# VectorE's attention loop written out, with the normalised row moved between the limit and the factors

## The reference

```
xm = exp(layer_norm(log(x)) * (1 + scale) + shift)
q, k, v = to_heads(exp(log(xm) @ w + b))          # 16 heads of 16, norms per head
out = exp(softmax(log(q) log(k)^T / 4) @ log(v))  # 64 x 64 scores per sequence and head
z = exp(log(from_heads(out)) @ w_o + b_o)
x1 = mobius_add(x, exp(gate * log(z)))
the same frame again around w_f1 and w_f2 (an MLP without an activation), then x + result
```

## Time and profile before

| what | us |
|---|---|
| time, median of three runs | 818.61 (817.21 to 820.23) |
| time of the profiled execution | 816.74 |
| its span, first to last instruction | 815.0 |
| DVE busy in the span | 671.9 (82%) |
| PE busy | 655.6 (80%) |
| ACT busy | 531.5 (65%) |
| POOL busy | 337.5 (41%) |
| mean granted clock of TensorE, share of full | 0.940 |

### The profile page before, as it was taken

The page is one execution under the profiler, slowest core; times in us unless marked ns, Lnnn a source line. Parts: engine busy times, 40 slices in busy tenths (PEclk is TensorE's granted clock), DMA queues, the critical chain, the costliest instruction groups (busy, mean ns, idle before and its releaser), DMA issues.

```text
span 815.0 us, 27718 instructions
## 1 busy us (share of the span) xinstructions
PE 655.6 (80%) x8355; PEld 468.1 (57%) x8369; DVE 671.9 (82%) x2230; ACT 531.5 (65%) x1563; POOL 337.5 (41%) x682
## 2 busy tenths in 40 slices
PE   5966988888888888888888887714669889989996
PEld 2655766666666666666666665502326556556654
DVE  2868898888889888888888898486997888888885
ACT  1125666667766666776666776334777888878884
POOL 1004555555555555555555555211233233134231
PEclk9979999999999999999999999555999999999999
DMA  9933755565555555565555654322443455445533
GB/s 322 357 98 89 137 130 119 131 134 124 134 129 129 123 129 134 123 133 118 129 128 125 133 132 98 76 65 65 117 117 102 125 150 155 131 130 155 152 96 104
DMA packets 184931, 107.53 MB, mean 132 GB/s; under 512 B 140202, under 2 KB 167730, under 8 KB 184883
## 3 DMA queue, kind: packets, MB, share of 16 engines
q1 hardware_dynamic: 183090, 104.11, 51.7%
q10 hardware_dynamic: 1792, 2.89, 1.0%
HBM read 64.24 MB, written 9.18 MB: 90 GB/s over the span
## 4 chain that ended last, share of the span: by engine, by line
DVE 34%; issue 29%; PE 15%; DMA 8%; DVEq 5%; ACT 4%; SPq 3%; POOL 2%; POOLq 0%; ACTq 0%
DVE hs L1151 7%; DVE lnx L1078 4%; PE p_s L948 3%; DVE g_all L1180 3%; DVEq L50 3%; SPq L365 3%; DMA mod_b<-mod_rows 2%; DMA qkT<-mod_b 2%; PE p_oz L859 2%; DMA x_all<-in_x 2%; PE p_qkv L948 2%; DVE fac L1200 2%; PE p_qkv L886 2%; DVE junk L1187 1%; PE p_t L934 1%
## 5 line engine op out<-in xcount | busy, mean ns | idle before, releaser
L886 PE MATMUL p_qkv<-wqkv,tT 128*128 128x256 f32 x768 | 197.2, 395 | 5.6 <-DVE u L1145 5.6
L886 PEld LDWEIGHTS p_qkv<-wqkv,tT 128*128 128x128 f32 x768 | 139.6, 195 | 22.8 <-issue 6.5
L859 PE MATMUL p_oz<-wo,oT 128*128 128x256 f32 x256 | 79.9, 439 | 6.0 <-ACT oT L624 0.5
L900 PEld LDWEIGHTS p_o<-v,pT 64*64 64x64 f32 x4096 | 67.9, 139 | 22.6 <-issue 22.6
L853 PE MATMUL p_oz<-ident,o 128*128 128x128 f32 x128 | 27.7, 300 | 63.4 <-DVE o L1165 55.1
L900 PE MATMUL p_o<-v,pT 64*64 64x17 f32 x4096 | 74.2, 211 | 0.0
L624 ACT ACTIVATE oT<-p_oz 128x256 f32<-128x256 f32 x64 | 24.6, 384 | 70.9 <-PE p_oz L853 70.9
L666 ACT ACTIVATE pT<-p_s 128x1024 f32<-128x1024 f32 x64 | 65.5, 1024 | 2.4 <-PE p_s L876 1.4
L1145 DVE SCALAR_TENSOR_TENSOR u<-p_qkv,ct,bqkv 128x768 f32<-128x768 f32 x64 | 64.4, 1006 | 3.2 <-PE p_qkv L886 3.2
L511 POOL TENSOR_TENSOR rt<-ss,c_mhalf 128x2 f32<-128x2 f32 x32 | 24.3, 760 | 101.7 <-ACT wqkv L714 99.0
L853 PEld LDWEIGHTS p_oz<-ident,o 128*128 128x128 f32 x128 | 13.3, 145 | 85.9 <-issue 80.7
(11 more groups left out here) (268 smaller groups left out, 1674.8 us busy)
## 6 DMA issues: line engine op xcount, KB each, us to landing
mod<-mod_rows SPq DMA_DIRECT2D x128, 128.0 KB, 2.8
x_all<-in_x SPq DMA_DIRECT2D x8, 1024.0 KB, 13.9
gate<-mod_rows SPq DMA_DIRECT2D x128, 64.0 KB, 2.8
mod<-mod_rows SPq DMA_DIRECT2D x32, 256.0 KB, 3.9
mod_b<-mod_rows SPq DMA_DIRECT2D x32, 256.0 KB, 4.0
out<-x_all SPq DMA_DIRECT2D x32, 256.0 KB, 2.2
gate<-gate_rows SPq DMA_DIRECT2D x32, 128.0 KB, 3.3
bqkv<-gate_rows SPq DMA_DIRECT2D x32, 128.0 KB, 3.8
```

The source lines that it names most:

```text
L859: mm = pe.matmul(p_oz[:, 0:D], oT[:, c, :, :].rearrange("p b s -> p (b s)"), wo[:, c, :], start=c == 0, stop=c == C - 1)
L886: mm = pe.matmul(p_qkv[:, a * D:a * D + D], tT[:, k, c, :], wqkv[:, c, a * D:a * D + D], start=c == 0, stop=c == C - 1)
L900: mm = pe.matmul(p_o[S * e:S * e + S, col:col + VW], pT[keys, e, g, :], v[keys, k, 2 * g + e, :], start=True, stop=True, skip_group_check= ...
```

## The change

VectorE's attention stage no longer has a loop: all 71 slots are written out, and the two halves of a slot are one function again. The other engines keep their loops. Inside the slot `modulate` moves from behind `scale_qk` to between `limit` and `factors`; `shift_t` stays behind `scale_qk`. No instruction of arithmetic is added or taken away.

```diff
-        def run_slots_rotated(eng, first_part, second_part, first, items, slots):
...
-            def slot_until_rows(h, off):
+            def slot(h, off):
                 if on(h, off, L_E):
                     limit(2 * h + off - L_E)
+                if on(h, off, L_A) and not at_start(h, off):
+                    modulate(2 * h + off - L_A, (off - L_A) % 2, h + (off - L_A) // 2)
+                if on(h, off, L_E):
                     factors(2 * h + off - L_E)
                     scale_qk(2 * h + off - L_E, (off - L_E) % 2)
-                if on(h, off, L_A) and not at_start(h, off):
-                    modulate(2 * h + off - L_A, (off - L_A) % 2, h + (off - L_A) // 2)
                 if on(h, off, L_A):
                     shift_t(2 * h + off - L_A, (off - L_A) % 2)
                 if on(h, off, L_D):
                     sum_squares(2 * h + off - L_D)
                     sum_rows(2 * h + off - L_D)
-
-            def slot_from_sums(h, off):
...
-            run_slots_rotated(dve, slot_until_rows, slot_from_sums, FIRST, T, T + L_G)
+            for s in range(T + L_G):
+                slot(s // 2, s % 2)
```

## The result

The changed kernel takes 786.61 us (median of 4 runs, 785.69 to 788.92) against 819.42 (817.21 to 821.41) of the kernel before: a ratio of 0.960, with a 95% interval of 0.957 to 0.964. The forecast was 797, in a range of 776 to 806. The profiled execution of after took 788.92, the slowest of its four runs; that of before, 816.74, was faster than every run that was timed beside after. The two spans are 787.1 and 815.0. In the changed kernel the lines of VectorE's stage stand 16 lower: the first copy is L1204, `z` L1157, `o` L1149, `u` L1129, the low half on GpSimd L469.

A forecast was written before the change was run, and what follows sets the result against it. VectorE's own list was taken to set the pace, plus a 2.71 us floor through PE. 55 slots falling from 7.07 to 6.70 save 20.4, plus 1.7, less 0.8: 21.3 off 816.74 is 795.4, plus 1.9 gives 797 us, range 776 to 806.

The forecast's parts named there:

- Writing out: VectorE's attention loop: without it, in the old order, a slot falls from 7.07 to 6.47 us, 0.60 less.
- The move: `modulate` ahead of `factors`: `z` to `o` falls from 3.74 to 3.56, but late `qk` delays copies; slot 6.70.
- The step after `limit`: VectorE with `modulate` behind `limit`: 0.12 us estimated from `limit` to `modulate`, part of `qk` at z + 1.10.
- Copy to `u`: VectorE, from first copy to `u`: 0.75 us beside GpSimd's v, read off slot 5, instead of 0.41.
- `u` to `z`: VectorE's end of a slot, from `u` to the end of `junk`: 1.81 us.
- The four slots with a late PE: Slots where VectorE waits for PE, 4.2 us in all: 1.7 us more saved, each still 0.62 over 6.70.
- Head and tail: Slots 7 and 63, slower by 0.25 and 0.23, and three pipeline-filling slots by about 0.1 each: 0.8 us back.
- From the profiled execution to the median: Step from one profiled execution to the runs: the median lies 1.9 us above, so 795.4 became 797.
- The copies don't wait: Rival: the chain over ScalarE and GpSimd tightens, slot between 6.27 and 6.47, time 779 us; chance 0.22.
- The 6.36 that I gave for a slot without contention: Slot time if VectorE's copies were not slowed by GpSimd's v: 6.36 us instead of 6.70.
- The chain grows: Rival: GpSimd or ScalarE lag 0.25 more each slot, slot 6.95, time 811 us, or 804 with half; chance 0.16.
- The mod row decides: Rival: `modulate` waits for its DMA row, slower than before from a landing of 4.65; 837 us at 5; chance 0.04.

The follow-up runs named there:

- e_order: The changed kernel with the old order (`modulate` behind `scale_qk` again), VectorE still written out: 781.89 us, ratio 0.956.
- e_four_slots: The kernel before, loop and old order kept, with four slots instead of two in each pass of VectorE's loop: 807.0 us, ratio 0.983.
- e_move_loop: The kernel before with its loop, and only `modulate` moved between `limit` and `factors`: 799.49 us, ratio 0.977.
- e_copies_late: The changed kernel with the two copies (`repeat_parts`) behind `project` (`u`) instead of ahead of it: 812.86 us, ratio 0.991.
- after_again: The changed kernel run once more, unaltered, beside another group of runs: 789.72 us, ratio 0.963.
- e_pool_flat: The changed kernel with GpSimd's slot loop written out as VectorE's is: 780.11 us, ratio 0.953.
- e_u3_late: The changed kernel with GpSimd's and ScalarE's attention loops written out too, the copies behind `project`, and a third buffer for `u`: 784.07 us, ratio 0.958.
- e_v_early: The changed kernel with GpSimd's v ahead of its low half instead of behind it: 795.93 us, ratio 0.974.
- e_sp_order: e_u3_late with SyncE written out and the gate row loaded ahead of the transpose, so the mod row goes out at once: 775.06 us, ratio 0.946.

## Why the prediction was right, and where its sizes were off

**Writing out, 0.60 a slot: right.** Slot 63 was what the writing out makes of every slot: 6.47 in e_order. The Trainium skill's rule (Advanced Engine Details and Errata, Control Flow Timing) priced the branch at 108 ns; the turn of the loop cost 0.54 with all that goes with it (e_four_slots), and what a looped slot has besides another 0.33. By that rule the writing out would have been worth 3 us, where the old order written out gained 37 (819.06 - 781.89).

**The move costs on balance: right, and by the mechanism named.** It saves DVE its own waits (`z` to `o` 3.49; forecast 3.56), makes `qk` late (z + 1.03; forecast z + 1.10), the low half with it, and the copies wait for that and then run beside v. Against e_order the move costs 0.14 a slot; the forecast had 6.70 - 6.47 = 0.23.

| step | forecast | measured | from |
|---|---|---|---|
| `qk` | z + 1.10 | z + 1.03 | 286.35 - 285.32 |
| low half starts, from `qk` | 1.78 | 1.78 | 281.51 - 279.73 (`qk` of that slot) |
| copies start | z + 4.14 | z + 4.03 to 4.06 | 289.35 - 285.32, 282.75 - 278.69 |
| copy to `u` | 0.75 | 0.84 | 283.59 - 282.75 |
| `u` to `z` | 1.81 | 1.73 | 285.32 - 283.59 |
| slot | 6.70 | 6.62 | 364.04 / 55 |

- *The step after `limit`.* I put 0.12 for it (between its busy time of 0.15, less some overlap, and 0.19), but an instruction that doesn't need the result before it follows `rlim` after 0.07, and `lnx` to `fac` is 0.39. So `qk`, and with it the copies, came 0.07 earlier.
- *Copy to `u`.* This went the other way. In slot 5 GpSimd idled behind v, and only the first copy was long. In after the small `nw` of L443 follows v at once, from 283.20 to 283.52. It runs already when the second copy starts at 283.31, and the copy ends 0.15 behind it, as the first does behind v: 0.36.
- *`u` to `z`.* I counted to the end of `junk`'s accumulator read, but `z` starts with that read (both at 285.32): 0.08 less.

Over 55 slots the difference is 4.4 us.

**The four slots with a late PE.** I let 2.5 of their 4.2 us stand. None is left: the granted clock of the stretch went from 0.98 to 1.00, and no `z` waits for PE. PE now idles 0.53 for `o`, where in the looped slots it was 0.73 and 1.27 in turn. In before such a slot is one of a low clock. Granted are 0.50 of full speed, the level of 1.2 GHz, from 140 to 142 us, and PE's projection takes 2.07 at 140.92 where it takes 1.13 at 148.67. All four come right behind an idle time of 1.27 or 1.28 ahead of the transpose of `o`. There are 26 such idle times in before and four slow slots; behind their first slots e_move_loop has 24 of about 1.2 and one slow slot, and e_copies_late mostly 0.9 to 1.0 and none. So it fits that the shorter idle time keeps the clock up, but most of the long ones have no such slot behind them, and no run changes the idle time alone. The miss is 2.5 us.

**Head and tail.** Forecast 0.8 lost, measured 0.85 and 0.2. That these are near each other is luck. I had slot 7 slower by 0.25, and it is slower by 0.05 (6.50); the other 0.80 lies ahead of it, and after_again, the same kernel, begins the stretch another 0.96 later, at 94.13. Together: 4.4 + 2.5 - 0.3 makes the 6.5 us between the forecast for the profiled execution, 795.4, and its 788.92.

**From the profiled execution to the median.** I carried over the 1.9 us (797.3, given as 797) by which the median of before lies above its profiled one. In after it is the other way round, 788.92 profiled against a median of 786.61. That is 4.2 us of the 10.4 by which the forecast was too high, and nothing of the kernel's: one execution lies above or below its median by chance, and the offset of one kernel doesn't carry over to another.

**Rivals.** "The copies don't wait" is refuted by the 0.2 ahead of them and the 640 ns; but its 779 is what e_pool_flat reaches (780.11), where the wait is all but gone (`o` to copy 0.38) and the copies stay at 0.64. The 6.36 that I gave for a slot without contention left something out: by my own times v ends at z + 4.66, and `u` has to wait for it, as e_copies_late shows, so it would have been about 6.5. "The chain grows" is refuted: `qk` to the low half is still 1.78. "The mod row decides" is refuted for after, where no `lnx` waits, and it is real all the same: e_u3_late shows it once the slot comes near 6.4, by 4.9 us over 13 slots. Its point of decision was put at a landing of 4.3; it came not by a longer landing but by a later issue, which I had held fixed.

**What I got wrong on the way.** e_move_loop (I held the move to be worthless in a loop), e_v_early and e_copies_late (both times a buffer that somebody still reads, seen only in the run), and the 6.20 for e_u3_late and e_sp_order, where I left out that `u` must wait for PE's products, which end 6.07 behind the transpose of `o` before them.

## What to carry to other kernels

Price a loop on an engine that sets the pace by a slot that is already written out in the same trace, and not by the branch: here the turn was 0.54 us a pass, and a looped slot cost 0.33 more besides. When an instruction is moved into a gap, follow what was behind the gap to the next engine and back; the same move gained 0.29 in the loop and lost 0.14 without it. Before two steps change places, ask for each of their buffers who reads it last.

## What the runs showed of the hardware

- An f16 copy of 128x512 on DVE takes 0.28 at least. One that starts while an instruction of GpSimd runs ends 0.15 behind that instruction: behind v in after (283.24 and 283.39) and in e_order (285.16 and 285.31), and behind the small step in after (283.52 and 283.67). All 118 copies of after from 92 to 480 us are within 0.03 of this. So 0.64 is no fixed price: the copy takes what is left of GpSimd's instruction and 0.15. If the copy is first, it keeps its 0.28 and GpSimd's step is the longer one (0.43 instead of 0.29 in e_v_early). By the Trainium skill's rule (GPSIMD Engine Reference, the row on SBUF interfaces) GpSimd shares them with VectorE, and contends with DVE instructions in a two-port mode or with two SBUF inputs. The trace agrees that the two contend; which of the conditions the copy meets, no run shows.
- `junk`'s accumulator read (0.08) and `z`, which doesn't need it, start together in after (both at 285.32), so there the read costs nothing.
- A wait put down to a DMA 51 times was a wait for ScalarE and for the engine's own register work. The engine named is the one whose event came last by the clock; where two come within some tenths of a us, the count that the kernel waits for, or a run that changes one of them, tells.
- A slot loop on GpSimd costs 0.19 between the release and the start of the released instruction (0.27 looped, 0.08 written out), which no list of waits shows, since it is counted with the wait for the other engine.
